# More products of constants in TensorE's queue: ahead of the bonus in the preparation of the scan, and at seven passages between stages

## What is computed

```python
a = jax.nn.sigmoid(time_aaaaa + a1 @ time_aaa_w2.T)
ma = jax.nn.sigmoid(time_misc_a + ma1 @ ma_w2.T)
k = k * ma + k * a * (1 - ma)
mk = jax.nn.sigmoid(time_misc_k + mk1 @ mk_w2.T)
k = k * jnp.exp(w * mk)
...
bonus = (r4 * k4 * time_faaaa.reshape(H, N)).sum(-1, keepdims=True) * v4
out = (yn + bonus).reshape(B, T, C) * g
```

## Time and profile before

| | us |
|---|---|
| median of 3 runs | 2860.07 |
| lowest, highest | 2855.85, 2862.87 |
| the profiled execution | 2858.35 |
| its span | 2856.4 |
| TensorE busy | 2418.9 (85%) |
| VectorE busy | 2147.7 (75%) |
| ScalarE busy | 1681.9 (59%) |
| mean granted clock of TensorE | 0.92 of full speed |

### The profile page before, as it was taken

How to read it: one execution, slowest core, us unless ns; L and a number is a source line. 1 busy time by engine, 2 the same in 40 slices (tenths; PEclk the granted TensorE clock), 3 DMA queues, 4 the chain that set the end, 5 groups by cost and what they waited for, 6 DMA issues and landing times. The chain is left out here.

```text
span 2856.4 us, 37348 instructions
## 1 busy us (share of the span) xinstructions
PE 2418.9 (85%) x10635; PEld 1074.2 (38%) x10730; DVE 2147.7 (75%) x5906; ACT 1681.9 (59%) x3069; POOL 1036.5 (36%) x1019
## 2 busy tenths in 40 slices
PE   6666378787888999989999989989988888879998
PEld 2211266664353434343333333333341111234443
DVE  6999589995686665565666656678569999758886
ACT  3445344543655666662222258855569999877775
POOL 1333489994144554430000034400030000028886
PEclk8788566768989999999999999999999999999999
DMA  3112575624185656442111123300031111101110
GB/s 135 59 59 74 135 136 110 114 42 126 49 260 112 131 108 127 78 155 71 36 36 34 35 54 91 91 2 0 1 116 44 46 40 46 29 24 41 45 45 26
DMA packets 297804, 211.74 MB, mean 74 GB/s; under 512 B 157640, under 2 KB 262008, under 8 KB 296952
## 3 DMA queue, kind: packets, MB, share of 16 engines
q1 hardware_dynamic: 258992, 189.78, 24.9%
q0 software_dynamic: 20352, 17.05, 4.1%
q10 hardware_dynamic: 18256, 2.52, 0.6%
HBM read 136.24 MB, written 62.52 MB: 70 GB/s over the span
## 5 line engine op out<-in xcount | busy, mean ns | idle before, releaser
L3221 ACT ACTIVATE ca_pw<-ca_ps,ca_mx 128x512 f32<-128x512 f32 x512 | 342.7, 939 | 7.3 <-DVE ca_mx L3257 7.3
L3257 DVE TENSOR_REDUCE ca_mx<-ca_ps 128x1 f32<-128x512 f32 x512 | 311.1, 673 | 0.7 <-PE ca_ps L3187 0.7
L3053 DVE CUSTOM_DVE_ANT_0 mx_sums<-mx_ps,w_w2f 128x384 f32<-128x384 f32 (+3 forms) x512 | 218.1, 486 | 112.2 <-PE mx_ps L3008 110.7
L2996 PE MATMUL gm_ps<-gm_h,w_w2f 128*128 128x512 f32 x512 | 239.0, 607 | 3.1 <-DVE gm_h L3081 3.1
L3221 ACT ACTIVATION_READ_ACCUMULATOR ca_pw<-ca_ps,ca_mx 128x1 f32 x512 | 234.9, 459 | 0.0
L3187 PE MATMUL ca_ps<-qs,ks 128*128 128x512 bf16 x484 | 172.1, 395 | 55.7 <-ACT ca_pw L3221 41.7
L2695 ACT ACTIVATE ta_pw<-ta_ps,w_cst 128x1280 f32<-128x1280 f32 x128 | 168.0, 1322 | 35.4 <-PE ta_ps L2572 35.1
L3125 ACT ACTIVATE gm_h<-gm_ps,w_w2f 128x512 f32<-128x512 f32 x64 | 44.0, 687 | 218.4 <-PE gm_ps L2996 218.4
L2827 DVE TENSOR_TENSOR ta_pw<-ta_pw,w_cst 128x384 f32<-128x384 f32 x128 | 70.7, 552 | 133.6 <-ACT ta_pw L2695 131.0
L2418 ACT ACTIVATE at_pw<-at_ps 128x1280 f32<-128x1280 f32 x128 | 157.1, 1238 | 19.2 <-PE at_ps L2384 19.0
L2740 POOL DMA_INDIRECT Acc<-XN,f_idx x64 | 103.7, 1620 | 155.8 <-DVE XN L2798 141.2
(11 more groups left out here) (594 smaller groups left out, 6272.6 us busy)
## 6 DMA issues: line engine op xcount, KB each, us to landing
Pd<-s_p SPq DMA_DIRECT2D x48, 384.0 KB, 5.0
ex_w<-e_w SPq DMA_DIRECT2D x48, 256.0 KB
Qd<-rp_q SPq DMA_DIRECT2D x4, 2048.0 KB, 7.6
ss_ellb<-Rd SPq DMA_DIRECT2D x32, 256.0 KB, 3.3
qs<-Pd SPq DMA_DIRECT2D x32, 192.0 KB, 4.2
ks<-Pd SPq DMA_DIRECT2D x32, 192.0 KB, 4.6
Pd<-cs_p SPq DMA_DIRECT2D x16, 384.0 KB, 2.4
GX<-Qd SPq DMA_DIRECT2D x44, 128.0 KB
```

Of the source, the lines that this page charges most:

```text
L2996: last = pe.matmul(at, W(("h1", "h2")[layer])[:, j * 512 + f * 128:j * 512 + (f + 1) * 128], (h0, h1)[layer][:, j, :], start=(j == 0), sto ...
L3053: return v.tensor_tensor_reduce(out=sums[:, bank, at:at + n], in0=ps[:, bank, at:at + n], in1=K["w2f"]("down")[:, T - n:T], scale=-1.0, sc ...
L3221: act.activation(pw[:, h % BUF, jk, :], ps[:, (h * NB + jk) % BANKS, :], ACT.Exp, bias=mx[:, h % H, jk:jk + 1], accum_out=z[:, h % H, jk:j ...
L3257: v.tensor_reduce(mx[:, h % H, jk:jk + 1], ps[:, q % BANKS, :], AX.X, ALU.max, negate=True).then_inc(S["top"], 1)
```

## The change

It adds calls of `kept_busy` and raises one count. In the preparation it adds 4 products ahead of the first mix of iteration 0 (the wait for `xxx` moves behind those for `q` and `v`), and in each of the four iterations 26 products between the value and the bonus, behind a wait for the last `mk` of the iteration, since the bank they write is read by the sigmoids until then. At the passages it adds 10 products at the end of the scan; 1, 1, 3 and 3 at the end of the choice; 6 at the start of layer 3's normalization; 5 at the end of the maxima; 5 more (13 for 8) and 3 in the row phase; 4 ahead of the first angles.

```diff
--- before.py
+++ after.py
@@ -287,9 +287,11 @@
             for i in range(IT):
                 t, ew, q = buffers(i)
                 for a in range(LANES):
-                    pe.wait_ge(S["xxx"][a], i + 1)
                     pe.wait_ge(S["q"][a], i)
                     pe.wait_ge(S["v"][a], i)
+                    if i == 0 and a == 0:
+                        kept_busy(pe, K, ps[:, 0, 0, :], 4)
+                    pe.wait_ge(S["xxx"][a], i + 1)
                     pe.matmul(ps[:, a, 0, :], W("maa_w1"), z[:, a, 0, :],
                               start=True, stop=True).then_inc(S["mixps"][a], 1)
                 if i:
@@ -332,6 +334,8 @@
                     pe.wait_ge(S["xv"][a], i + 1)
                     pe.matmul(ps[:, a, 0, :], W("value"), xf[:, a, 3, :],
                               start=True, stop=True).then_inc(S["vps"][a], 1)
+                pe.wait_ge(S["mk"][LANES - 1], i + 1)
+                kept_busy(pe, K, ps[:, LANES - 1, 1, :], 26)
                 for a in range(LANES):
                     pe.wait_ge(S["rk"][a], i + 1)
                     pe.matmul(ps[:, a, 1, :], cst("headsum"), t[:, a, 0, :],
@@ -660,6 +664,7 @@
             sums(LOTS - 2)
             sums(LOTS - 1, LOW)
             sums(LOTS - 1, HIGH)
+            kept_busy(pe, K, tps[:], 10)
 
         @block.vector
         def _(v):
@@ -1384,16 +1389,21 @@
                         total(N * b + k - EARLY)
             for n in range(N * B - EARLY, ROUNDS):
                 total(n)
+            pe.wait_ge(S["r"], N * B)
+            kept_busy(pe, K, ps[:, 0, :], 1)
             pe.wait_ge(P["eqn"], 1)
             pe.wait_ge(P["need"], 1)
             pe.matmul(tot, cst("exbefore"), cnt[:], start=True, stop=True).then_inc(P["off"], 1)
+            kept_busy(pe, K, ps[:, 0, :], 1)
             pe.wait_ge(P["last"], 1)
             pe.wait_ge(P["rank"], 3)
             pe.matmul(tot, cst("exbefore"), cnt[:], start=True, stop=True).then_inc(P["off2"], 1)
+            kept_busy(pe, K, ps[:, 0, :], 3)
             pe.wait_ge(P["pos"], 1)
             for n in range(2):
                 last = pe.transpose(turned[:, n, :], m[:, 0, n * 128:(n + 1) * 128], cst("ident"))
             last.then_inc(P["turned"], 1)
+            kept_busy(pe, K, ps[:, 0, :], 3)
 
         @block.scalar
         def _(act):
@@ -1904,6 +1914,7 @@
                     pe.wait_ge(S["ln"], b - 3)
                 pe.matmul(variances(b), cst("mean"), GX[:, batch(b)], start=True, stop=True).then_inc(S["var"], 1)
 
+            kept_busy(pe, K, mps[:, 0, :], 6)
             for t in range(B if gated else B + 2):
                 if t < B:
                     mean(t)
@@ -3045,6 +3056,7 @@
                             turned(i - 1)
                         scores(i, g, r)
             turned(B - 1)
+            kept_busy(pe, K, ps[:, 0, :], 5)
 
         @block.vector
         def _(v):
@@ -3323,7 +3335,7 @@
                 if t >= 2:
                     squares(B + t - 2)
             pe.wait_ge(S["ln"], 2 * B)
-            kept_busy(pe, K, sps[:, 0, :], 8)
+            kept_busy(pe, K, sps[:, 0, :], 13)
             pe.wait_ge(P["ell"], 1)
             pe.wait_ge(P["gam"], 1)
             pe.wait_ge(P["bd"], 1)
@@ -3331,6 +3343,7 @@
                 for j in range(NB):
                     last = pe.transpose(cps[:, n, j, :], q[:, n, j * 128:(j + 1) * 128], cst("ident")[0:HB, 0:HB])
             last.then_inc(P["cps"], 1)
+            kept_busy(pe, K, sps[:, 0, :], 3)
 
         @block.scalar
         def _(act):
@@ -3593,6 +3606,7 @@
                 if i + 1 < B:
                     turned(i + 1)
 
+            kept_busy(pe, K, ps[:, 0, :], 4)
             pe.wait_ge(S["dx"], 1)
             angles(0)
             first_gate(0)
```

## The result

The changed kernel took 2890.18 us in the median of 4 runs (2887.05 to 2893.18), the kernel before 2858.78 us beside it (4 runs, 2855.85 to 2862.87): a ratio of 1.0108, with a 95% interval of 1.0095 to 1.0121. It is about 31 us slower; 2890.4 us was forecast. The profiled execution has a span of 2885.3 us, 28.9 more than before, at a mean granted clock of 0.94 where it was 0.92. TensorE is at the full clock more often, and the kernel is slower.

A forecast was written before the change was run, and what follows sets the result against it. VectorE was taken to set the pace in the preparation, TensorE's speed counting only where VectorE or a barrier waits. The terms 16.2 + 4.7 + 3.3 + 0.8 + 2.5 + 2.8 = 30.3 us gave 2890.4 us, range 2879 to 2900.

The forecast's parts named there:

- The price of a product: One filler product is two records, 0.86 us at the full clock and 1.7 us cold.
- Rival (a): The products fit into the idle time ahead of the bonus and only the passages cost: 2874 us; 5%.
- Part 1: Preparation: 26 products ahead of the bonus, four times, make VectorE and finally GpSimd wait: +16.2 us (13.5 to 20).
- Part 2: End of the scan: 10 products make TensorE end later and delay the next stage: +4.7 us (3 to 4.9).
- Part 3: End of the choice: 1, 1, 3 and 3 products delay L1389, L1395 and the stage's end: +3.3 us (2 to 5.5).
- With one of them cold: End of the choice: one of the three products ahead of L1395 runs cold, making it 2.6 us late.
- Part 4: Ahead of layer 3's first mean: 6 products delay it, the warm clock paying two thirds: +0.8 us (0.6 to 0.9).
- Part 5: End of the maxima: 5 products, four records of them cold, delay the next stage: +2.5 us (1.1 to 2.8).
- the warm one: End of the maxima: all products at the full clock, so the next stage starts only 1.1 us late.
- Part 6: Row phase and first angles: 13 for 8, then 3, then 4 products: +2.8 us (1.5 to 6).
- Rival (c): Warmth pays more than the waits, mainly in the preparation, so not slower: about 2855 us; 4%.
- Rival (d): The change does nothing, since TensorE's idle time covers all the products; 3%.

The follow-up runs named there:

- runs 3: Kernel before with only 14, 19 or 36 products added ahead of the bonus: 2857.59, 2860.39 and 2907.29 us (the last from one execution).
- run 4: run 2 with other counts: scan end 3, choice 0, 0, 3, 3, maxima 10, layer 3's means 3, row phase 13 and 0; 2867.42 us.
- run 2: Changed kernel without the 26 products ahead of the bonus, so the passages alone: 2871.32 us, ratio 1.0048 to the kernel before.
- run 5: Kernel before with 4 products added between the dots and the deltas in iterations 1 to 3: 2859.14 us, ratio 0.9996.
- run 6: Changed kernel with every call cut to its idle time (14 ahead of the bonus) and 4 products ahead of the deltas: 2857.73 us, ratio 1.0002.

## Why the prediction was right, and where its terms were off

**The price of a product** held: 52 records in 22.59 us, and 0.86 us for each further product in runs 3 (bonus) and 4 (maxima). Rival (a) rested on a cheaper one and falls.

**Part 1** was 16.2 us; it cost 18.1 (17.6 alone). VectorE's wait (5.3 forecast, 5.4 measured), lane 1's z (0.7, 0.83) and iterations of 4.3 us (4.4 and 4.5) hold; so does GpSimd's L269 as the last link (+3.2, +3.4). The term that was off is the one put at nothing for the deltas' products. I took their clock to be the same with the change, since the idle time ahead of them is. But behind 4.04 to 4.06 us of idle time their 16 records took anything from 3.35 to 3.80 us. In the changed kernel iteration 2 had a slower set than before, and VectorE's waits were 1.2 us longer. That the products cause this is not shown: run 4 has a slow set in the same iteration with nothing ahead of the bonus. Runs 3 with 14 and 19 products have the same look: counted from L215 of iteration 0 the next stage starts 1.6 and 1.3 us later than before with hardly a new wait at L215 (L164 waits 2.4 and 2.7 us in all, 1.7). Without the 1.3 us of iteration 2 part 1 is 16.8 us, against 16.2 forecast; whether the 1.3 belong to the change stays open. The 4 products ahead of the first mix cost nothing, as forecast: in run 2, which has them, L215 of iteration 0 starts at 107.03 us (before 107.07).

**Part 2**, +4.7: the table has 4.4 and 3.8, but that holds the scatter of the scan; from the last sums to the next stage's first transfer it is 4.2 us both times. The order of events (products, barriers, next stage) is as forecast. The stage starts 1.7 us behind TensorE's last record, where I had taken the 2.3 us that lay behind the store's DMA.

**Part 3**, +3.3 within 2 to 5.5: measured 4.9 and 5.2. "With one of them cold" was mis-sized: the three ahead of L1395 take 4.59 us, about two of them at 1.2 GHz, and L1395 is 3.7 us later from there on and not 2.6. I had let the two single products raise the clock, by the 3.4 us that I read off the long call in the earlier trace rows. Here TensorE was busy for all of 868 to 872 us and the clock stayed at 0.50, and the first four of the six records behind were slow as well. That reading holds for its own call and is no rule.

**Part 4**, +0.8: measured 0.8 twice. With 3 products it is -0.3. The mean starts 1.8 us later and the full clock gives back 1.0 of it, rather less than the two thirds that I wrote.

**Part 5**, +2.5 within 1.1 to 2.8: measured 1.1 twice. Of my two cases the warm one came. I chose by a mean clock of 0.75 over 1670 to 1671 us, a stretch in which TensorE was idle for half of the time. With products directly behind the transposes the clock did not fall.

**Part 6**, +2.8: measured 3.3 twice. The stage starts 2.1 us later, not 1.5, since the 13 products and the three behind the transposes take 0.5 us more than I gave them. Of the 1.3 us at the angles less is the products' doing than the table suggests: in four of the six other kernels without them VectorE was 1.0 to 1.5 us late there too, waiting for the transfer. In the three kernels with them it waits for TensorE and is 1.3 us late each time. Where VectorE waits for the transfers it starts 0.1 us behind the last of the four landings. By that, an estimate from the landing times in the traces, the products cost 0.4 us at this point in the changed kernel, 1.2 in run 2 and 0.7 in run 4.

The parts as measured add to 32.6 us in the changed kernel's trace, which is only 28.9 longer. The difference lies in stretches that the change leaves alone, and these scatter: the stage behind the choice took 361.8 to 367.1 us over the ten traces, in no order that follows the products. Run 2, which has the same products at the passages, gave nothing back in these stretches together, so this is scatter and no payment; for a single stretch, other than the stage behind the choice, it is only likely.

The mechanism of the forecast is right, and that its sum of 30.3 us came within about 1 us of the 31 measured is partly luck: parts 1, 3 and 6 were too low by 4.0 us together, parts 2 and 5 too high by 1.7, and the times themselves are known to some 4 us.

**Rival (c)**, that warmth pays, is answered by runs 3, 5 and 6: the warm bonus alone gives nothing that can be measured, the warm deltas at most 1.0 us of 2859. Raising the mean clock from 0.92 to 0.94 without making anything late in the stages (run 6) changed the time by 0.02%, with an interval of -0.08% to +0.13%. The Trainium skill ("TensorE: Matmul & The Clock Gate", "What's actually happening") says that the ramp is under 1% of a typical kernel's span. Run 6 is in keeping with that and does not show it, since most of the slow stretches of this kernel were left as they were. Rival (d) falls with the waits at L215.

## What to carry to other kernels

Price a filler product from the trace, in its own type and shape, and compare it with the room up to the point where the next engine wants the result, not with TensorE's idle time up to its own next instruction: here 14.2 us of idle time took 19 products (16.6 us) for nothing, and seven more cost some 18 us over four iterations. At the end of a stage there is no such room once TensorE is the last at the barrier; each product there is paid in full. And before filling a wait, ask who waits for the operation behind it: before the change the slow clock of the bonus cost nothing, and in the runs with 14 and 19 products its faster clock won nothing.

## What was not expected of the hardware

A product that comes 2 us behind 12.3 us of products at the full clock can be at 1.2 GHz: with 14 products, lane 0's bonus took 1.83, 1.13, 1.12 and 1.72 us in the four iterations, and lane 1's, after 1 to 1.7 us more of idle time, 2.07 or 2.08 each time; in run 6, also with 14, lane 1's was once at 1.13. Products that end right at the work (19, 26 or 36) left it at the full clock, 1.02 us in every iteration. And four transfers of 64 KB at the start of the last stage were issued in 1.70 us in some executions and in 3.19 in another, by the same queue with the same work.
